# Another order ahead of the first conv step of a gated SSM and mixture-of-experts block: D on another queue, the second group's x and statistics later, Hankel parts of two, two, four and eight heads

## The reference, cut to what matters

```
kv  = einsum('bhil,bhjl->bijhl', ctx, ctx)            # 16 heads of 8 rows
y   = causal convolution of kv with ssm_kernel[h]     # along l, 256 taps
out = y + kv * D[h]
out = einsum('bijhl,bhil->bjhl', out, layernorm(x))
x   = x + tanh(g_xattn) * out
```

## Time and profile before

| | |
|---|---|
| median of three runs | 349.8 us (349.69 to 349.81) |
| profiled execution, its span | 362.1 us |
| busy, PE / PE's weight loads | 309.8 us (86%) / 255.4 us (71%) |
| busy, DVE / POOL / ACT | 212.3 us (59%) / 197.5 us (55%) / 124.6 us (34%) |
| memory traffic | 36.83 MB read, 26.81 MB written |

### The profile page before, as it was taken

One profiled execution on the slowest core, in us unless ns is written; L12 is line 12 of the kernel. 1 busy time (PEld: TensorE's weight loads), 2 busy tenths in 40 slices (PEclk: granted clock), 3 DMA queues, 4 the chain that ended last, 5 costly groups with the idle time before them and its releaser, 6 DMA issues.

```text
span 362.1 us, 5101 instructions
## 1 busy us (share of the span) xinstructions
PE 309.8 (86%) x1578; PEld 255.4 (71%) x1578; DVE 212.3 (59%) x522; ACT 124.6 (34%) x353; POOL 197.5 (55%) x232
## 2 busy tenths in 40 slices
PE   3898767899999899978939949999999998999860
PEld 1898756789988689857727636677777676776850
DVE  3689984877699896796054211132433443478286
ACT  2438346822772006630456000333122332432000
POOL 2899967384888668827744750022514433684200
PEclk9999969699999999996978988999999999999895
DMA  5989999820111201104981013057769999679796
GB/s 178 292 280 297 268 369 359 225 78 32 65 57 44 67 32 62 57 16 136 276 241 43 2 37 95 0 155 169 171 142 275 277 310 228 104 106 256 192 339 216
DMA packets 52890, 59.27 MB, mean 164 GB/s; under 512 B 6618, under 2 KB 48470, under 8 KB 52864
## 3 DMA queue, kind: packets, MB, share of 16 engines
q1 hardware_dynamic: 42336, 47.24, 43.8%
q0 software_dynamic: 7248, 8.56, 12.3%
q10 hardware_dynamic: 3280, 3.15, 2.6%
HBM read 36.83 MB, written 26.81 MB: 176 GB/s over the span
## 4 chain that ended last, share of the span: by engine, by line
PE 39%; DVE 20%; DMA 15%; issue 15%; another core or an unknown queue 5%; ACT 2%; SPq 2%; POOL 1%; DVEq 0%; ACTq 0%; POOLq 0%
DMA expert_sum<-arena,ide 9%; PE pg L1058 8%; PE pu L1058 7%; DVE arena L777 5%; PE Y L1046 3%; PE Y L1210 3%; PE Y L1048 3%; PE Y L1047 3%; PE pu L1089 3%; DVE arena L769 3%; DMA shared<-expert_sum 2%; PE pg L1089 2%; DMA arena<-in_ctx_dram 2%; DVE arena L766 2%
## 5 line engine op out<-in xcount | busy, mean ns | idle before, releaser
L472 POOL DMA_INDIRECT expert_sum<-arena,ide x29 | 45.0, 1552 | 79.0 <-DVE arena L957 58.6
L395 POOL DMA_INDIRECT dispatched<-rows,dsu x64 | 63.7, 995 | 34.0 <-issue 19.4
L385 POOL TENSOR_TENSOR arena<-arena 128x256 f32<-128x256 f32 x96 | 57.8, 638 | 4.3 <-ACT arena L486 3.9
L1046 PE MATMUL Y<-arena 128*128 128x192 f32 x128 | 33.8, 347 | 9.3 <-DVE arena L769 9.3
L777 DVE TENSOR_REDUCE arena<-arena 128x128 f32<-128x1024 f32 x32 | 38.7, 1211 | 0.2
L943 DVE TENSOR_TENSOR arena<-arena,Y 128x176 f32<-128x176 f32 x32 | 10.8, 338 | 47.1 <-ACT arena L683 45.3
L676 ACT ACTIVATE arena<-Y,wn 128x128 f32<-128x128 f32 x64 | 20.0, 364 | 44.2 <-PE Y L1201 37.6
L549 ACT ACTIVATE silu<-pg 128x512 f32<-128x512 f32 x20 | 11.9, 595 | 61.4 <-PE pg L1058 61.4
L1048 PE MATMUL Y<-arena 128*128 128x192 f32 x128 | 32.7, 339 | 0.0
L1047 PE MATMUL Y<-arena 128*128 128x192 f32 x128 | 32.7, 339 | 0.0
L787 DVE TENSOR_TENSOR act<-silu,pu 128x512 f32<-128x512 f32 x20 | 13.7, 684 | 30.9 <-PE pu L1058 18.3
(11 more groups left out here) (179 smaller groups left out, 641.4 us busy)
## 6 DMA issues: line engine op xcount, KB each, us to landing
dispatched<-zrow SPq DMA_DIRECT2D x1, 4624.0 KB, 21.4
arena<-dispatched SPq DMA_DIRECT2D x32, 144.5 KB
expert_sum<-zrow SPq DMA_DIRECT2D x2, 2176.0 KB, 17.5
shared<-expert_sum SPq DMA_DIRECT2D x8, 512.0 KB, 7.3
arena<-in_L_ffn_w_gate_dram SPq DMA_DIRECT2D x22, 176.0 KB
arena<-in_L_ffn_w_up_dram SPq DMA_DIRECT2D x22, 176.0 KB
arena<-in_L_ffn_w_down_dram SPq DMA_DIRECT2D x22, 176.0 KB
arena<-taps SPq DMA_DIRECT2D x4, 512.0 KB, 5.9
```

Of the source, the lines that this page charges most:

```text
L385: ins = pool.tensor_tensor(o[:, :, blk], i0, i1, ALU.mult)
L395: pool.indirect_dma_start(buf, bass.IndirectOffsetOnAxis(ap=dsu[:, t % 2, j:j + 1], axis=0), rows[:, t % 2, j // K, :], None, bounds_check ...
L472: pool.indirect_dma_start(accs[a], bass.IndirectOffsetOnAxis(ap=ide[:, e % NO:e % NO + 1], axis=0), ye[:, e % NO, :], None, compute_op=ALU ...
L1046: pe.matmul(yv[:, 0], TT[:, h, P:L], kvv[:, 0], start=True, stop=True)
```

## The change

D's load goes from SP to ACT, as ACT's first. SP issues the Hankel matrix in parts of 2, 2, 4 and 8 heads; x of the second group goes behind the first two parts, its ctx behind the third, and the fourth part comes after the ctx. PE waits for each part at its first head. The warm-up transposes are six instead of ten, and group 1's transposes stand behind conv steps 3 to 6. DVE does group 1's statistics behind multiplication 0 and its coefficients behind reduction 1. POOL does the products of steps 0 to 3, then `query_pow(1)`, then those of steps 4 to 7, and its constants after them.

```
--- before.py
+++ after.py
@@ -30,7 +30,7 @@
 ACCR = B * S + CAP
 KPAD = 384
 KVR = 8
-HPARTS = 4
+HEADS_IN = (2, 2, 4, 8)
 NPRE, NW, NX, NO = 5, 16, 8, 8
 OPEN, CLOSE, OWN = 15, 24, 3
 ADDED = E - OWN
@@ -45,7 +45,7 @@
            (2, 0): 2, (2, 1): 3, (2, 2): 4, (2, 3): 5, (2, 4): 6, (2, 5): 7, (2, 6): 8, (2, 7): 9,
            (3, 0): 10, (3, 1): 11, (3, 2): 12, (3, 3): 13, (3, 4): 14, (3, 5): 15, (3, 6): 16, (3, 7): 17}
 LATE = 18
-WARM = 10
+WARM = 6
 UNITS_EXPERT = range(32, 40)
 
 
@@ -227,7 +227,7 @@
         x_sem = [sem(f"x_in{g}") for g in range(G)]
         ctx_sem = [sem(f"ctx_in{i}") for i in range(GB)]
         disp_sem = [sem(f"dispatched{t}") for t in range(G)]
-        hankel_sem = [sem(f"hankel_in{i}") for i in range(HPARTS)]
+        hankel_sem = [sem(f"hankel_in{i}") for i in range(len(HEADS_IN))]
         gu_sem = [sem(f"gate_up_weights_in{i}") for i in range(NW)]
         wd_sem = [sem(f"down_weights_in{i}") for i in range(NW)]
         xe_sem = [sem(f"xe_in{i}") for i in range(NX)]
@@ -258,13 +258,12 @@
         @block.sync
         def _(sp):
             sp.dma_start(k_raw, ssm_kernel).then_inc(s["ker_in"], 16)
-            sp.dma_start(d_sb[:], ssm_D.rearrange("(h o) -> h o", o=1)).then_inc(s["ker_in"], 16)
-            load_x(sp, 1)
             sp.wait_ge(s["taps_ready"], 1)
             sp.dma_start(scratch_k, kp).then_inc(s["taps_out"], 16)
             sp.wait_ge(s["taps_out"], 16)
-            for i in range(HPARTS):
-                h0, hn = i * H // HPARTS, H // HPARTS
+
+            def load_hankel(i):
+                h0, hn = sum(HEADS_IN[:i]), HEADS_IN[i]
                 sp.dma_start(TT[:, h0:h0 + hn, :],
                              bass.AP(scratch_k.tensor, scratch_k.offset + h0 * KPAD, [[1, P], [KPAD, hn], [1, L]])
                              ).then_inc(hankel_sem[i], 16)
@@ -274,7 +273,12 @@
                     sp.wait_ge(s["k_tr"], t - GB + 1)
                     load_ctx(sp, t)
 
+            load_hankel(0)
+            load_hankel(1)
+            load_x(sp, 1)
+            load_hankel(2)
             more_ctx(1)
+            load_hankel(3)
             sp.dma_start(gates[:, 0:1], g_xattn.partition_broadcast(P)).then_inc(s["gate_in"], 16)
             sp.dma_start(gates[:, 1:2], g_ffn.partition_broadcast(P)).then_inc(s["gate_in"], 16)
             sp.dma_start(wr[:, :, 0:E], w_router.rearrange("(p c) e -> p c e", c=2)).then_inc(s["wr_in"], 16)
@@ -407,21 +411,20 @@
                                    ).then_inc(s["xnT_low"], 1)
 
             query_pow(0)
-            products(0, 0)
-            products(0, 1)
+            for p in range(4):
+                products(0, p)
+            query_pow(1)
+            for p in range(4, NP_):
+                products(0, p)
             link(pool.memset(ones[:], 1.0))
             link(pool.affine_select(out=tri[:], in_=ones[:], compare_op=ALU.is_gt, fill=0.0, base=0,
                                     pattern=[[1, P]], channel_multiplier=-1))
-            query_pow(1)
-            products(0, 2)
             link(pool.iota(iota_e[:], pattern=[[1, E]], base=0, channel_multiplier=0, allow_small_or_imprecise_dtypes=True))
             link(pool.iota(slot0[:], pattern=[[CAP, E]], base=0, channel_multiplier=0, allow_small_or_imprecise_dtypes=True))
             link(pool.iota(limit[:], pattern=[[CAP, E]], base=CAP, channel_multiplier=0, allow_small_or_imprecise_dtypes=True))
             link(pool.iota(tok[:], pattern=[[S, B]], base=0, channel_multiplier=1, allow_small_or_imprecise_dtypes=True))
             link(pool.tensor_copy(carry[:], slot0[:]))
             pool.sem_inc(s["consts"], 1)
-            for p in range(3, NP_):
-                products(0, p)
             for p in range(4):
                 products(1, p)
             query_pow(2)
@@ -475,6 +478,7 @@
 
         @block.scalar
         def _(act_e):
+            act_e.dma_start(d_sb[:], ssm_D.rearrange("(h o) -> h o", o=1)).then_inc(s["ker_in"], 16)
             load_x(act_e, 0)
             for b in range(GB):
                 load_ctx(act_e, b)
@@ -749,7 +753,6 @@
                 dve.tensor_scalar(q_st[:, b].rearrange("p (c l) -> p c l", c=2)[:, :, ::-1],
                                   x_tile(0, b).rearrange("p (c l) -> p c l", c=2), mvq[:, b, 0:1], rq[:, b:b + 1],
                                   ALU.subtract, ALU.mult).then_inc(s["q_ready"], 1)
-            q_stats(1)
 
             def mult(g, p):
                 k = NP_ * g + p
@@ -884,11 +887,14 @@
                     dve.wait_ge(disp_sem[t - 2], 16 * GB * K)
                 dve.tensor_copy(dsu[:, t % 2], dst[:].rearrange("p b k -> p (b k)")).then_inc(s["dst_ready"], 1)
 
-            q_coef(1)
             for p in range(NP_):
                 mult(0, p)
+                if p == 0:
+                    q_stats(1)
                 if p:
                     reduce(0, p - 1)
+                if p == 2:
+                    q_coef(1)
             dve.wait_ge(s["consts"], 1)
 
             for g in range(1, G):
@@ -1039,8 +1045,9 @@
                     pe.wait_ge(s["q_evac"], 2 * k + 2)
                 for hh in range(2):
                     h = 2 * p + hh
-                    if g == 0 and h % (H // HPARTS) == 0:
-                        pe.wait_ge(hankel_sem[h // (H // HPARTS)], 16)
+                    for i in range(len(HEADS_IN)):
+                        if g == 0 and h == sum(HEADS_IN[:i]):
+                            pe.wait_ge(hankel_sem[i], 16)
                     yv = Y[:, 2 * (p % 2) + hh, :].rearrange("l (c b n) -> l c b n", c=2, b=GB)[:, :, :, 0:48]
                     kvv = kv[:, p % KVR].rearrange("m (c b h) n -> m c b h n", c=2, b=GB)[:, :, :, hh]
                     pe.matmul(yv[:, 0], TT[:, h, P:L], kvv[:, 0], start=True, stop=True)
@@ -1148,9 +1155,9 @@
                 pe.transpose(pg[:, 0:P], ident[:], ident[:])
             for p in range(NP_):
                 conv(0, p)
-                if 1 <= p < 5:
-                    k_tr(1, p - 1)
-                    q_tr(1, p - 1)
+                if 3 <= p < 7:
+                    k_tr(1, p - 3)
+                    q_tr(1, p - 3)
             conv(1, 0)
             for g in range(1, G):
                 t = g - 1
```

46 lines of the change are left out of this document (26 added, 20 removed).

## The result

The changed kernel takes 355.94 us (median of four runs, 352.91 to 358.7) against 349.81 us: ratio 1.0154, 95% interval [1.0098, 1.021]. The execution of 358.7 us counts as a slow one, and the ratio leaves it out; the median of the other three is 354.42 us. The sign was forecast, the size not: 351.3 us, range 348.7 to 354.4. Its profiled execution took 357.45 us, span 355.7 us.

The account below looks back on a forecast made before the run. DVE was taken to bound the first group, DVE and POOL arriving together at the tokens' power; after the change POOL alone decides. xn transposes +1.95, clock -0.45: +1.5 us, 351.3 us, range 348.7 to 354.4.

Parts of the forecast that it names:

- the path: Late second-group transposes delay ACT's copy, then POOL by 5.1 us; POOL alone decides the tokens' power, at 50.2.
- the wait for q: PE stands 2.4 us before the second group's first q transposes, which need ACT's query and its coefficients.
- ACT's copy late: ACT's copy of the second group's last k half comes at 31.3 instead of 25.56.
- POOL idle: POOL waits 3.9 us for ACT's copy before its first product of the second group, at 31.6 instead of 26.5.
- The constants' new place: POOL does its constants after the first group's last products, ending at 27.7, before waiting for the copy.
- SP's later issue: Later loads on SP's queue issued up to 5.5 us later, priced at nothing; 5 us if their cover were gone.
- the store behind the power: 2.2 us between rows ready (50.3) and used (52.55) on PE; xn transposes move only +1.95, to 54.5.
- 0.45 us off for the clock: At full clock, PE's two sets of four from the xn transposes on cost 0.45 us less.
- the front: Multiplication 0 at 13.95, 1.44 us sooner; moved statistics spend the front's gain: 0, bounds -0.5 and +0.5.
- the price of six warm-ups: Six warm-up transposes on PE end at 11.8, so step 0 starts 0.8 us sooner than 12.60.
- the mark that I had set at 1 us from 23: On DVE, the forecast counts as wrong if multiplication 3 starts 1 us from 23.
- Rival B: PE's clock falls at the first new wait, making DVE and POOL late: +4.4 us, 354.2; chance 0.17.

Follow-up runs that it names:

- late transposes and POOL's waits: Kernel before, second group's transposes behind conv steps 3 to 6, POOL waiting for its own subtractions after each four: 353.87 us, ratio 1.0173.
- second trace of before: The kernel before, unchanged, profiled once more: execution of 350.13 us, span 348.4 us; runs beside it had a median of 348.56 us.
- kernel before with POOL's waits: Kernel before, POOL waiting for its own subtractions after the fourth and the eighth: 347.2 us, ratio 0.9971.
- ten warm-ups: Changed kernel with ten warm-up transposes instead of six: runs of 353.29, 355.5 and 359.26 us, one stray of 1055, no ratio.
- POOL's waits: Changed kernel, POOL waiting for its own subtractions after the fourth and the eighth: 357.83 us, ratio 1.0244.
- variances late: Changed kernel, the first tokens' variance instructions moved on DVE behind the second group's multiplication 2: 356.69 us, ratio 1.0224.
- late transposes alone: Kernel before, only the second group's transposes moved behind conv steps 3 to 6 instead of 1 to 4: 354.53 us, ratio 1.020.
- power at 46.69: Changed kernel, POOL's eight subtractions moved behind the first tokens' power, POOL waiting for them after each four: 352.46 us, ratio 1.0127.
- statistics late without POOL's new order: Kernel before, second group's transposes behind steps 2 to 5, its statistics behind multiplication 0, coefficients behind reduction 1: 363.19 us, ratio 1.0432.

## Why the prediction was wrong

**Right: the path.** The question was put to the right place. Transposes late, the wait for q (2.64 us; 2.4 forecast), ACT's copy late, POOL idle (6.20; 3.9 forecast) and from there on POOL as what decides the tokens' power: each row is there, and in the table the last conv step follows the power. The constants' new place, which the sum gave no price, costs nothing that the runs show. That SP's later issue costs nothing is not shown; no run separates it.

**Failed step 1: the store behind the power.** I let 4.9 us of a later power become 1.95 us at the xn transposes, since the rows were ready at 50.3 and used at 52.55, and took 0.45 us off for the clock. The size of that term is the largest miss that does not hang on one execution's clock. Measured, 8.5 us of power (53.75 against 45.28) became 7.5 at the xn transposes, 7.25 at top-k and 6.0 to 7.5 at the last conv step; there is a store of about 1 us, not 3. The kernel with late transposes and POOL's waits suggests why: the xn transposes do come 4.49 us behind the power (I had 4.3) and only 0.4 us later than in the second trace of before, just as I reckoned, but PE has stood idle for them, runs at half clock, and top-k is 1.4 us later. The 0.45 us did not come back either: from the xn transposes to the next conv step it takes 2.52 us there, 2.42 before. The slack of before was PE at work; when it was used up, PE stood idle and its clock fell. Four traces show this idleness and this fall (above). It is no law: in the kernel before with POOL's waits the xn transposes also come 4.50 us behind the power, PE is idle for only 0.38 us ahead of them, and its clock stays up. Where DVE was held (the changed kernel), conv step 4 came late itself and the slack stayed in its place, 6.33 us from power to xn. The prediction has no hold of DVE at all, but the traces of the late transposes with and without it differ by only 0.4 us at the last conv step. From power to top-k it is 12.64 us in the changed kernel; with that, my own power at 50.2 gives top-k at 62.84, +3.7 against 59.14 where I had +1.5. In the three traces of this front in which the clock held at the wait for q (ten warm-ups, POOL's waits, variances late) the power is 1.0 to 1.6 us later than I had it, and top-k, at 63.45 to 64.60, is 2.8 to 4.0 us later than 59.14 + 1.5.

**Failed step 2: the front, 1.8 us.** Multiplication 0 at 15.78, not 13.95 (14.55 to 15.62 in the seven other kernels made from the changed one). I let POOL's first products start 1 us sooner and called it a gain. They started at 8.09, over DVE's writing of q, which took 2.74 us instead of 1.38. Other traces grade it: POOL at 8.97, 2.00 us; at 9.16, 1.68; at 9.46 or later, 1.38. PE's q transposes end later by it, and conv step 0 ran with the long instructions, which the price of six warm-ups left out. So multiplication 3 was at 24.75, not 23.0; the mark that I had set at 1 us from 23 was passed. POOL's first product of the second group, 5.1 us later by the forecast, was 8.5 us later, of which this step and the clock are 3.2; in the five traces with the clock up it was 5.9 to 6.7.

**Rival B, 1.4 us, in this execution.** The clock did fall at the wait for q, which I gave 0.17: conv step 4 at 0.85 us each, and multiplication 4 3.2 us behind the forecast, 1.75 of it the front's. In five other kernels the same wait left the clock up, with ten warm-ups and with six. So this part is true of the trace and is not the change's price; what decides it is open.

Together, in this trace: the forecast's 1.5, the store that wasn't there 2.2 (the remainder, not a measurement of its own), and a power 3.55 us later than forecast (the front 1.8, the clock 1.4, and 0.35 that I can't place): 7.25, the shift of top-k (66.39 for 59.14). The medians differ by 6.1.

**What stays open.** The sum of the experiments' parts isn't closed: the late transposes alone cost 6 us by the runs (354.53 against 348.42) but 2.2 at the last conv step, one trace against one. 1.6 us of the difference may be that the second trace of before is of a long execution; single executions of the kernel before ran from 345.3 to 353.1 us. The 1.3% that are left with the power at 46.69 are more than its 1.7 us of delay accounts for. The warm-ups and the change's own transfers have no run whose time tells their price. And POOL's waits removed a hold at a place where their own hole does not lie; I did not find out by what means.

## What to carry to other kernels

Where two engines arrive at a point together, ask of each what makes it late, and take a delay of either as passed on nearly whole (7.25 of 8.5 us here). Slack read between two rows on PE may be work that keeps its clock up, and is not to be spent at face value. A fall of the clock seen in one trace is first to be looked for in the traces of kernels that are the same up to there. A stream without a hole on POOL is a resource of DVE's too: look in the view by line for instructions whose longest is thirty times their median, and count one as a loss only if something waits for it; ahead of the join taking it away moved the last conv step by 0.4 us, behind it by 3.9 us for 2.9 us of hold and by 5.3 for 6.8. A part moved alone can cost more than the whole change (statistics late without POOL's new order, 4.3%): parts that feed each other are to be undone together.
